# A two-layer attention and feed-forward kernel: nine ring places, slot rows turned at stage 3, weights rounded by halves, one norm and count for the last two batches

## The reference, cut to what matters

```python
x = x + cross_attention(layernorm(x), ctx, Wq, Wk, Wv, Wo, bo)    # 16 batches, 112 tokens, 16 heads of 64; 375 context rows
x = x + routed_ffn(layernorm(x))      # relu(xf@sw1+sb1)@sw2+sb2 for all, and of two experts the one with the larger gate score;
                                      # the expert not chosen sees zeros and still adds relu(b1)@w2 + b2
x = x + masked_attention(layernorm(x), ctx, ctx)   # one head of 256, row mask
x = x + int8_linear(layernorm(x))     # quantised by the largest |x| of all, weight_int8, scale, bias
```

## Time and profile before

| | us |
|---|---|
| median of 3 runs (lowest to highest) | 1006.86 (996.07 to 1007.52) |
| the profiled execution, its own time | 1006.59 |
| its span, first to last instruction | 1004.8 |
| PE busy / DVE / ACT / POOL | 922.9 / 632.9 / 524.9 / 284.3 |
| mean granted TensorE clock | 0.963 of full |

### The profile page before, as it was taken

The page is one execution under the profiler, slowest core; times in us unless marked ns, Lnnn a source line. Parts: engine busy times, 40 slices in busy tenths (PEclk is TensorE's granted clock), DMA queues, the critical chain, the costliest instruction groups (busy, mean ns, idle before and its releaser), DMA issues.

```text
span 1004.8 us, 19746 instructions
## 1 busy us (share of the span) xinstructions
PE 922.9 (92%) x6695; PEld 804.7 (80%) x6695; DVE 632.9 (63%) x1637; ACT 524.9 (52%) x1246; POOL 284.3 (28%) x346
## 2 busy tenths in 40 slices
PE   6889999999999999999999999987799999987754
PEld 5778889888988898889888988866688889964443
DVE  5856666765766767657667676566555554575357
ACT  4655556565555555655555555534524453563313
POOL 1323333342424333424333333224210000510004
PEclk9999999999999999999999999998999999997785
DMA  9320000000000000000000000013322300634412
GB/s 279 112 78 17 1 22 15 5 20 0 20 15 5 20 15 5 20 0 20 15 5 20 15 5 5 1 64 114 104 79 97 126 19 19 186 95 125 129 49 73
DMA packets 29459, 50.56 MB, mean 50 GB/s; under 512 B 2480, under 2 KB 24080, under 8 KB 27648
## 3 DMA queue, kind: packets, MB, share of 16 engines
q1 hardware_dynamic: 27888, 46.42, 15.1%
q0 software_dynamic: 1536, 3.67, 1.2%
HBM read 41.83 MB, written 8.26 MB: 50 GB/s over the span
## 4 chain that ended last, share of the span: by engine, by line
PE 84%; DVE 9%; issue 3%; ACT 3%; DMA 1%; SPq 0%; POOL 0%; DVEq 0%; ACTq 0%
PE bank L1609 26%; PE bank L1638 9%; PE bank L1657 8%; PE bank L1802 8%; PE bank L1623 7%; PE bank L1821 7%; PE bank L1591 6%; PE bank L1678 5%; PE bank L1887 3%; PE bank L1905 2%; DVE hid_lo L1372 1%; DVE down_lo L995 1%; PE bank L1773 1%; DMA wq_sb<-in_wq 1%; PE bank L1570 1%
## 5 line engine op out<-in xcount | busy, mean ns | idle before, releaser
L633 POOL TENSOR_TENSOR probs<-probs,row_rcp 112x375 f32<-112x375 f32 x256 | 202.4, 813 | 418.5 <-DVE row_rcp L1100 418.0
L775 ACT ACTIVATE probs<-bank,neg_max 112x375 f32<-112x375 f32 x256 | 144.4, 569 | 72.6 <-DVE neg_max L1094 72.6
L1638 PE MATMUL bank<-ident,probs 112*125 112x112 f32 x768 | 129.0, 277 | 4.8 <-DVE probs_t L1105 4.8
L1638 PEld LDWEIGHTS bank<-ident,probs 112*125 112x125 f32 x768 | 113.9, 188 | 21.7 <-issue 5.7
L1094 DVE TENSOR_REDUCE neg_max<-bank 112x1 f32<-112x375 f32 x256 | 123.3, 539 | 6.0 <-PE bank L1623 5.8
L1105 DVE COPY probs_t<-bank 125x336 f32<-125x336 f32 x128 | 64.6, 506 | 69.5 <-PE bank L1638 65.3
L1609 PE MATMUL bank<-ctx_hi,wk_hi 128*128 128x376 f32 x256 | 97.5, 381 | 2.1 <-DVE k_parts L1085 1.8
L747 ACT ACTIVATE k_parts<-bank 128x376 fp32r<-128x376 f32 x128 | 62.1, 485 | 69.6 <-PE bank L1609 69.5
L1657 PE MATMUL bank<-probs_t,v 125*64 125x112 f32 x1536 | 87.7, 263 | 0.6 <-ACT probs_t L763 0.6
L1085 DVE TENSOR_TENSOR k_parts<-bank,k_parts 128x376 fp32r<-128x376 f32 x128 | 69.9, 547 | 28.6 <-ACT k_parts L747 28.4
L750 ACT ACTIVATE v<-bank 125x512 f32<-125x512 f32 x96 | 57.4, 598 | 58.4 <-PE bank L1609 58.4
(11 more groups left out here) (187 smaller groups left out, 1950.6 us busy)
## 6 DMA issues: line engine op xcount, KB each, us to landing
stage<-in_ffn_up SPq DMA_DIRECT2D x6, 1024.0 KB, 4.8
stage<-in_ffn_down SPq DMA_DIRECT2D x6, 1024.0 KB, 5.4
ctx_raw<-in_ctx_t SPq DMA_DIRECT2D x16, 375.0 KB, 3.4
stage<-in_ctx_t SPq DMA_DIRECT2D x8, 375.0 KB, 7.0
stage<-in_ctx_n SPq DMA_DIRECT2D x8, 375.0 KB
ring_more<-in_ctx_t SPq DMA_DIRECT2D x8, 375.0 KB, 7.3
ring_more<-in_ctx_n SPq DMA_DIRECT2D x8, 375.0 KB
routed<-xn SPq DMA_DIRECT2D x1, 2240.0 KB, 9.5
```

The costliest lines, as they stand in the source:

```text
L633: eng.tensor_tensor(probs[s][:, :], probs[s][:, :], row_rcp[:, s:s + 1].broadcast_to([S, C]), ALU.mult).then_inc(probs_ready, 1)
L775: eng.activation(probs[r][:, :], SCORE_BANKS[i][0:S, 0:C], ACT.Exp, bias=neg_max[:, r:r + 1], accum_out=row_sum[:, r:r + 1]).then_inc(exp_ ...
L1638: t = eng.transpose(turn_bank(i, project)[0:CJ, j * S:(j + 1) * S], probs[QUAD * v + i][:, j * CJ:(j + 1) * CJ], ident[0:S, 0:S])
```

## The change

- The ring of the second attention has nine places instead of four. Places 0 and 1 (the stage buffers) are loaded when all weights are split, places 2 to 6 behind the slot before last and its store, 7 and 8 after the last slot's store; batch t waits for batch t-9.
- The next slot's rows are turned at stage 3 (rest at 4) except before the first slot, where they are turned at 6 instead of 5; the last result is turned at stage 5 (copied out at 6), or at 4 in segments 1 and 8. The turn of the result waits for the rows' rest, as both use bank 7.
- Weights are rounded and subtracted in halves, one half a stage. The first experts' pieces go to (0,6) and (0,7), (1,0) and (1,1), (1,3) and (1,4), (2,1) and (2,2); later ones to stages 3 to 6.
- Batches 14 and 15 share one norm (stages 0 to 3 of segment 0), gate and turn (stage 4) and count (stages 4 and 5); the last scatter goes ahead of `idle_sum`; the total is counted at (0,6); the idle products and `expert_biases` move from (2,2) to (2,7).
- `split_shared(0)` goes from the last half's first visit to the half before. SP's order up to `load_chosen(0)` and what `idle_sum` waits for are not changed.

```diff
-        ring_more = [sb(f"ring_more{i}", [P, JT * D + KT * CP]) for i in range(2)]
+        ring_early = [sb(f"ring_early{i}", [P, JT * D + KT * CP]) for i in range(2)]
...
-        ring = [stage[0][:, :], stage[1][:, :], ring_more[0][:, :], ring_more[1][:, :]]
+        ring_late = [sb(f"ring_late{i}", [P, JT * D + KT * CP]) for i in range(5)]
+        ring = [r[:, :] for r in stage + ring_late + ring_early]
+        NR = len(ring)
...
-        Y_OUT, TURN_Y, Y_ROWS, TURN_ROWS, SPLIT_ROWS = 1, 3, 4, 5, 6
+        Y_OUT = 1
+        def turn_y_stage(s):
+            return 4 if s + 1 == FIRST_SLOT or s == NS - 1 else 5
+        def turn_rows_stage(s):
+            return 6 if s + 1 == FIRST_SLOT else 3
...
-        SPLIT_AT = {(0, 3): EXPERT_PIECE, (0, 5): EXPERT_PIECE + 1, (1, 1): EXPERT_PIECE + 2,
-                    (1, 4): EXPERT_PIECE + 3}
-        for i in range(CHOSEN):
-            SPLIT_AT[FIRST_SLOT + 1 + i, 3] = CHOSEN_PIECE + 2 * i
-            SPLIT_AT[FIRST_SLOT + 1 + i, 5] = CHOSEN_PIECE + 2 * i + 1
+        SPLIT_AT = {}
+        for s0, m0, i in ((0, 6, 0), (1, 0, 1), (1, 3, 2), (2, 1, 3)):
+            for h in range(2):
+                SPLIT_AT[s0, m0 + h] = (EXPERT_PIECE + i, h)
+        for i in range(2 * CHOSEN):
+            for h in range(2):
+                SPLIT_AT[FIRST_SLOT + 1 + i // 2, 3 + 2 * (i % 2) + h] = (CHOSEN_PIECE + i, h)
+        def piece_half(t, h):
+            n = t.shape[1] // 2
+            return t[:, h * n:(h + 1) * n, :]
+        def hi_halves(i):
+            return i if i < FFN_PIECE else FFN_PIECE + 2 * (i - FFN_PIECE)
...
+            def load_ring(t):
+                r = t % NR
+                if t >= NR:
+                    eng.wait_ge(energy_ready, t - NR + 1)
+                eng.dma_start(ring_t[r][:, :, 0:C], ctx_t[t]).then_inc(ring_t_loaded[r], 16)
+                if t >= NR:
+                    eng.wait_ge(mix_ready, t - NR + 1)
+                eng.dma_start(ring_n[r], ctx_n[t].rearrange("(j p) d -> p j d", j=JT)).then_inc(ring_n_loaded[r], 16)
...
+            eng.wait_ge(weights_split, len(PIECES))
+            load_ring(0)
+            load_ring(1)
+            eng.wait_ge(down_ready, FIRST_SLOT + SLOTS - 1)
...
+            for t in range(2, 2 + len(ring_late)):
+                load_ring(t)
+            eng.wait_ge(down_ready, FIRST_SLOT + SLOTS)
...
-            def load_ring(t):
-                if t >= 4:
-                    eng.wait_ge(energy_ready, t - 3)
-                eng.dma_start(ring_t[t % 4][:, :, 0:C], ctx_t[t]).then_inc(ring_t_loaded[t % 4], 16)
-                if t >= 4:
-                    eng.wait_ge(mix_ready, t - 3)
-                eng.dma_start(ring_n[t % 4], ctx_n[t].rearrange("(j p) d -> p j d", j=JT)) \
-                   .then_inc(ring_n_loaded[t % 4], 16)
-            eng.wait_ge(weights_split, len(PIECES))
-            eng.wait_ge(down_ready, FIRST_SLOT + SLOTS)
-            for t in range(B):
+            for t in range(2 + len(ring_late), B):
...
+            scatter(B - 1, xn[0])
...
-                if e == 0:
-                    eng.wait_ge(place_ready, B)
-                    scatter(B - 1, xn[0])
...
-            def piece_hi(i):
+            def piece_hi(i, h=None):
...
+                    eng.activation(hi, place, ACT.Copy).then_inc(weights_hi, 1)
...
                     eng.wait_ge(stage_loaded[i % 2], 16 * ((i - FFN_PIECE) // 2 + 1))
-                eng.activation(hi, place, ACT.Copy).then_inc(weights_hi, 1)
+                    for k in range(2) if h is None else (h,):
+                        eng.activation(piece_half(hi, k), piece_half(place, k), ACT.Copy).then_inc(weights_hi, 1)
...
-                        i = SPLIT_AT[s, m]
+                        i, h = SPLIT_AT[s, m]
...
-                        piece_hi(i)
-                    if s == 0 and m == 7:
-                        tokens_out(1, B - 1, bank[6])
+                        piece_hi(i, h)
+                    if s == 0 and m == 5:
+                        for j in range(2):
+                            tokens_out(1, B - 2 + j, bank[6][:, KT * S * j:KT * S * (j + 1)])
...
-                    if m == Y_ROWS and is_slot(s - 1):
+                    if m == turn_y_stage(s) + 1 and is_slot(s - 1):
...
-            def piece_lo(i):
+            def piece_lo(i, h=None):
...
-                eng.wait_ge(weights_hi, i + 1)
-                eng.tensor_tensor(lo, place, hi.bitcast(F32), ALU.subtract).then_inc(weights_split, 1)
+                if i < FFN_PIECE:
+                    eng.wait_ge(weights_hi, i + 1)
+                    eng.tensor_tensor(lo, place, hi.bitcast(F32), ALU.subtract).then_inc(weights_split, 1)
+                else:
+                    for k in range(2) if h is None else (h,):
+                        eng.wait_ge(weights_hi, hi_halves(i) + k + 1)
+                        o = eng.tensor_tensor(piece_half(lo, k), piece_half(place, k), piece_half(hi, k).bitcast(F32),
+                                              ALU.subtract)
+                        if k == 1:
+                            o.then_inc(weights_split, 1)
...
-                        if last and c == 1 and v == 0:
+                        if last and c == 0 and v == 1:
+                            eng.wait_ge(proj_ready[0], unit_count(u + 1, 4))
...
+            LAST = slice(B - 2, B)
...
-                base = (2 + NORM_OPS) * (B - 1)
+                base = (2 + NORM_OPS) * (B - 2)
...
-                    gate_choice(B - 2, xn[1])
+                    norm_stats(norm2, 0, B - 2)
...
-                    norm_stats(norm2, 0, B - 1)
-                    eng.wait_ge(norm2.step, base + 1)
-                    norm_moments(norm2, 0)
-                if 2 <= n < 5:
-                    done = 5 * (n - 2)
-                    for i in range(done, min(done + 5, NORM_OPS)):
-                        norm_op(norm2, base + 2, i, slice(0, 1))
-                if n == 3:
-                    find_place(B - 2, bank[6])
+                    norm_stats(norm2, 1, B - 1)
+                    eng.wait_ge(norm2.step, base + 2)
+                    for j in range(2):
+                        norm_moments(norm2, j)
+                if 2 <= n < 4:
+                    done = 7 * (n - 2)
+                    for i in range(done, min(done + 7, NORM_OPS)):
+                        norm_op(norm2, base + 4, i, slice(0, 2))
+                if n == 4:
+                    eng.wait_ge(norm2.step, base + 4 + NORM_OPS)
+                    eng.wait_ge(scattered, 16 * (B - 2))
+                    for j in range(2):
+                        normalise(1, norm2, B - 2 + j, j, xn[1 - j])
+                    for j in range(2):
+                        eng.wait_ge(xn_ready[1], B - 1 + j)
+                        eng.wait_ge(gate_summed, B - 2 + j)
+                        eng.scalar_tensor_tensor(out=gate_work[0:S, :], in0=xn[1 - j], scalar=1.0, in1=gate_row[:, :],
+                                                 op0=ALU.mult, op1=ALU.mult, accum_out=gate_sum[:, j:j + 1]) \
+                           .then_inc(gate_summed, 1)
+                    eng.wait_ge(gate_summed, B)
+                    eng.tensor_scalar(chosen[:, :], gate_sum[:, :], 0.0, None, ALU.is_gt).then_inc(chosen_ready, 1)
...
-                    eng.wait_ge(norm2.step, base + 2 + NORM_OPS)
-                    normalise(1, norm2, B - 1, 0, xn[0])
-                    gate_choice(B - 1, xn[0])
+                    eng.tensor_tensor(offset[:, :], chosen[:, :], from_end[:, LAST], ALU.mult).then_inc(rank_ready, 1)
+                    eng.wait_ge(counted, B - 1)
+                    eng.tensor_tensor(rank[:, :], token[:, LAST], MISC_BANK[0:S, 0:2], ALU.subtract) \
+                       .then_inc(rank_ready, 1)
+                    eng.wait_ge(rank_ready, B)
+                    eng.tensor_tensor(place[:, LAST], offset[:, :], rank[:, :], ALU.add).then_inc(place_ready, 1)
...
-                    find_place(B - 1, MISC_BANK)
...
-                    eng.tensor_scalar(second[:, i:i + 1], MISC_BANK[:, 0:1], float(B * S - GT * (i + 1)), None,
+                    eng.tensor_scalar(second[:, i:i + 1], MISC_BANK[:, 2:3], float(B * S - GT * (i + 1)), None,
...
-                    if (s, m - 1) in SPLIT_AT:
-                        piece_lo(SPLIT_AT[s, m - 1])
+                    if divmod(n - 1, MT) in SPLIT_AT:
+                        piece_lo(*SPLIT_AT[divmod(n - 1, MT)])
...
-                    if s == FIRST_SLOT and m == 2:
+                    if s == FIRST_SLOT and m == 7:
...
-                    if m == Y_ROWS and s >= 1 and not is_slot(s - 1):
+                    if m == turn_y_stage(s) + 1 and s >= 1 and not is_slot(s - 1):
...
-                    if m == SPLIT_ROWS and is_slot(s + 1):
+                    if m == turn_rows_stage(s) + 1 and is_slot(s + 1):
...
+                if s == FIRST_SLOT + 2:
+                    eng.wait_ge(b2_ready, 1)
...
-                y_rows_free(s - 2)
```

(44 more changed lines are left out.)

51 lines of the change are left out of this document (25 added, 26 removed).

## The result

The kernel before took 1004.67 us in the median of four runs (996.07 to 1007.52) and the changed kernel 992.41 (991.05 to 997.19). The ratio is 0.9883, with a 95% interval of 0.9835 to 0.9932: 1.2% faster, by 12 us, which lies within the 2% that the prediction called no change. The profiled execution of the changed kernel took 991.05 us, with a span of 989.3.

What follows compares the result with a forecast made beforehand. TensorE, 84% of the chain, was taken as the bound, so savings count only where it waits or runs slowly. -4.5 + 1.1 + 3.3 + 6.9 + 0.6 + 5.2 - 27.3 = -14.7 from 1006.6 gave 991.9, in round 992; range 980 to 1004.

Steps and rivals of the forecast that it cites:

- Last batch: Last attention batch: -4.5 us, as the split and norm steps ahead of DVE's last maxima leave; bounds -1.5 and -5.5.
- Segment 0: +1.1 us: port conflict and two splits go; waits of 4.2 at the gate and 2.5 at end, slow clock 1.5.
- Segment 1: +3.3 us: expert-choice wait goes, but PE waits up to 8.9 for rows behind POOL and piece 4; 35.4 against 32.1.
- The sign that was named: Sign that the forecast is right: PE waiting some 9 us at L1784 in segment 1 for rows issued after POOL's L674.
- Segment 2: +6.9 us: POOL's idle sum holds up DVE, so `turn_y(1)` costs PE 5.6, with 2.3 slow clock; bounds 0 and 9.
- The open question of whether a rounding is held: Segment 2: whether POOL also holds the rounding of (2,4); if not, 3.6 of the 6.9 us go.
- Segments 3 to 5: +0.6 us: a wait of about 1.5 leaves the end; a new 1.7 stands at stage 5, three times; bounds -4.5, +6.
- Segment 8: +5.2 us: answers copied out 4.9 later, fewer ring loads give back 1.2, PE waits 3.7, clock 1.5; bounds 0 and 8.
- Rival (3): Ring loads still come late, sharing SP's queue with the answers; half of 18.2 us stays, 1004 us; chance 0.06.
- Second attention: -27.3 us: 18.2 of ring-load waits go, PE then binds; 59.7 against 87.0, including 4.4 for DVE and ACT.
- rival (2): Second attention stays at 1.2 GHz, a batch about 5 us instead of 3.12; 1011 us with 10 batches; chance 0.11.
- Rival (1): New waits cheaper: rounding not held (-3.6), clock holds at (0,4) and segment 8 (-3.0), DVE keeps up (-4.4); 981; chance 0.27.

Runs made afterwards that it cites:

- the two kernels that divide the change: The changed kernel with only four ring places, 1016.07 us (ratio 1.011), and the kernel before with the nine places alone, 982.08 us (0.977).
- The swapped order: Changed kernel with the rounding of the next slot's rows ahead of the half piece on ScalarE and VectorE in slot segments; 991.04 us (0.9872).
- the kernel with four places: Changed kernel with only four ring places, loaded behind the last store, all other parts kept; 1016.07 us (1.011).
- that with the loads behind, the other: Changed kernel with ring places 4 to 6 loaded behind the store of the last slot's answers instead of ahead; 989.93 us (0.9828).
- the last kernel: Changed kernel with both edits at the last slot, rows ahead of piece 4, rows before half pieces, idle sums split, `split_shared(1)` at stage 6; 971.94 us (0.9634).
- one edit alone: Changed kernel with the last slot's answers turned at stage 3 of segment 7 instead of stage 5; 994.08 us (0.9871).
- in quarters of POOL's work: Changed kernel with POOL's multiply of the idle sums issued as four instructions and its first add as two; 991.75 us (0.9892).
- the kernel with both edits at the last slot: Changed kernel with last slot's answers turned at stage 3 of segment 7 and only ring places 2 and 3 loaded ahead of their store; 984.45 us (0.9829).

## Why the prediction was right, and where its steps were off

The forecast was 992.0 and the median is 992.41. The sum was right for the reason given, a large gain in one stage less a row of losses in others, and the two kernels that divide the change show both parts: 24 us off by the ring, 10 us back by the rest. The forecast had them as 27.3 and 12.6. It put all of the last segment's loss on the rest; the ring has a part of its own there, and its 24 us are 30 in the second attention less 4.6 in segment 8, to within 1.4. Three of the terms were off by 2 us or more.

**Last batch.** -4.1 against -4.5. The 2.81 wait of the earlier trace rows is gone, those of 0.36, 1.21 and 0.63 are as before, and the window has the full clock.

**Segment 0.** +1.9 against +1.1. The two waits named are there: 2.24 and 0.45 us around the gate and count, and 2.36 at up(1,0), forecast at 2.5. The term for the slow clock, 1.5, was 2.5 (last section). (The sum written there, 19.0 + 4.2 + 2.5 + 1.5, is 27.2 and not 27.3.)

**Segment 1.** The step by which the wait for the expert choice "goes" failed: it is still 2.36 us. The choice was to be "made a stage and a half before it is asked for"; in the trace DVE begins it at 702.01 and PE asks at 703.49, 1.5 us later, and POOL begins in between, at 702.17, with `which` behind it at 702.32. The prediction knew of the hold ("The DVE work that the port holds up meanwhile hides in it", that is, in the wait for the rows), but took the choice as made before POOL starts. The other half, rows that wait behind POOL and piece 4, held: forecast 20.7 us from up(1,2) to rows landed, measured 19.9 (697.13 to 717.04). That the wait for them was 3.19 and not 8.9 is because PE came 5 us later, by the waits for `which` and `hid_lo`; the three together are 7.3. The term came out 2.1 too high, since the slow clock behind them was smaller in this execution (0.95). In five other kernels with this segment unchanged it took 33.7 to 36.3 us, 35.3 in the mean, which is the forecast's 35.4; the 33.3 of this execution is the lowest of the six. The sign that was named, PE waiting some 9 us for rows, did not show: the delay was there but lay in three waits.

**Segment 2.** The mechanism was right: `turn_y(1)` waits 4.98 us (5.6 forecast) for the rows' rest, behind a rounding of 2.91 and a `hid_lo` of 2.64 us, and the kernel without the idle sums has 0.45 in its place. The open question of whether a rounding is held is answered with yes. Under the Trainium skill's "SBUF — State Buffer", section "Who interferes with whom", a cast in a 2-port mode and an operation with two SBUF inputs are shut out for the whole of a GpSimd instruction that was issued first, and one with a single SBUF input outside those modes is not; the cast's 2.91, the `hid_lo` and the unheld `xs_lo` from PSUM agree with it. The term was 1.8 too high, in its clock part: 2.3 us of new slow clock were forecast, and PE was busy 24.2 us where it had been 24.0.

**Segments 3 to 5.** +0.5 against +0.6, with three waits of 1.58 (1.7). The swapped order shows the half piece as their cause.

**Segment 8.** Here a term was mis-sized: 5.2 forecast, 11.2 measured, and its upper bound of 8 did not hold. "The last slot's answers are copied out two stages later, 4.9 us" was right. "Fewer ring loads run beside the gathers, which gives back 1.2" looked at the wrong transfer. The loads stand in front of the store, not beside the gathers, and the store waited 3.6 us more for them (7.9 against 4.3); the kernel with four places and that with the loads behind show 4.0. Rival (3) had seen that ring loads and answers share SP's queue, but only asked whether the loads would be late. With both, 4.9 and 3.6, PE's wait was 8.24 instead of 3.7, and the slow clock behind it cost 2.9: in the last kernel the same segment takes 23.84 us, which with 8.24 makes 32.1 of the 35.0.

**Second attention.** -30.0 against -27.3. The clock is 1.00 and PE's 51.85 us of work bound it, so rival (2), the slow clock there, is out. The 4.4 us taken for DVE and ACT are 5.2 of waits for ACT; with PE's work that is the 57.0. The term was too small a gain because PE's work was taken as 53.1 (49.9 and 3.2) and 2.2 us were added for the ends, of which nothing is left.

**Rival (1)**, cheaper new waits, did not happen: the rounding was held, the clock fell behind the waits at (0,4) and in segment 8, and of the third condition there is only that the second attention was 2.7 us shorter than forecast, with the waits for ACT all there. Rival (3) is out for the loads themselves.

Terms too low by 6.0 (segment 8), 0.8 and 0.4 stood against ones too high by 2.1, 1.8, 2.7 and 0.1; that, 2.05 us less in the first attention, which isn't explained, and 0.8 more in the tail put the profiled time 0.9 us under the forecast. The closeness of the total is partly luck: the terms are off by 14 us in all when added without their signs.

## What to carry to other kernels

A change that moves a store and adds loads has to be read along the queue that issues both: count what stands ahead of the store when it is ready, for an early store may meet a fuller queue. Of two delays in one chain, one edit alone took nothing off the segment and the other 3.2 us, and both together took off 10.4, so a small effect of one edit doesn't clear its cause. And when a change has one large gain and several small prices, run the large part alone: here it was 10 us better than all of it.

## What the runs showed that was not expected

- A conversion of 128x3 elements on DVE took 3.48 us and three products of 128x8 took 3.72 together beside POOL's two-input operations; in quarters of POOL's work the conversion took 0.92. The same conversion took 0.17 in the kernel before, beside no POOL instruction. In these rows it isn't the number of elements of DVE's instruction that sets its time but the length of POOL's.
- In the changed kernel SP took 0.55 and 0.58 us to issue the first transfer of ring places 2 and 3 and 4.15, 3.35 and 3.74 us for that of places 4 to 6. The second load of the same places took 0.5 to 0.8 us throughout. In these rows the engine that issues is itself held, and with it whatever else it has to issue.
- The clock behind the same wait differs from run to run. After the 2.24 us at stage 4 of segment 0 the changed kernel ran at 0.55 from 678.0 to 684.0, and the segment took 28.06 us; the kernel with both edits at the last slot, with the same instructions there, ran at full clock after it and took 25.57:

```profile
678.00:684.00 6.00, 5.97 (x21) 5.42 (x22) 0.00 (x0) 0.65 (x2) 0.00 (x0) 0.55 0.01 3
```

```profile
665.75:691.32 25.57, 20.26 (x111) 17.60 (x109) 12.28 (x40) 12.22 (x21) 2.65 (x3) 1.00 0.38 113
```

  Of the eleven kernels with this segment as the change has it (the changed one and ten of the twelve), three had the short form in the profiled execution, 25.6 us, and eight the long one, 27.9 to 28.1. Such a stretch cost the segment some 2.4 us, as much as several of the edits gained. It isn't simply saved where it is missing: in the kernel with both edits the clock was 0.69 from 691.5 to 697.0, behind the next wait, and segments 0 and 1 took 61.0 us together against 61.4 in the changed kernel. So edits of this size are to be read from their waits and not from the total.
